# Transposes of x1 as pairs of 64 rows, and the issue of loads and stores exchanged between GpSimd and SyncE

## The reference, cut to what matters

```python
x = x + L0_conv(gn(x))     # 3x3 convolution of int8-valued x and weights, with bias
x = x + L1_conv(gn(x))     # keep 2*16 x 16 low frequencies of rfft2, mix channels, irfft2
```

## Time and profile before

| what | value |
|---|---|
| median of 3 runs | 3610.84 (3604.45 to 3612.75) |
| the profiled execution, its own time | 3599.9 |
| its span | 3598.1 |
| TensorE, matmuls busy | 3060.9 (85%) |
| VectorE busy | 3091.9 (86%) |
| ScalarE busy | 2371.9 (66%) |
| GpSimd busy (DMA issues among it) | 695.4 (19%) |
| DMA traffic | 1352.57 MB, mean 376 GB/s |
| chain that ended last, largest parts | TensorE 44%, DMA 41%, VectorE 6% |

### The profile page before, as it was taken

One profiled execution on the slowest core, in us unless ns is written; L12 is line 12 of the kernel. 1 busy time (PEld: TensorE's weight loads), 2 busy tenths in 40 slices (PEclk: granted clock), 3 DMA queues, 4 the chain that ended last, 5 costly groups with the idle time before them and its releaser, 6 DMA issues.

```text
span 3598.1 us, 81875 instructions
## 1 busy us (share of the span) xinstructions
PE 3060.9 (85%) x33273; PEld 1524.8 (42%) x33273; DVE 3091.9 (86%) x3288; ACT 2371.9 (66%) x3523; POOL 695.4 (19%) x1040
## 2 busy tenths in 40 slices
PE   5666666599999999999999999688888888888886
PEld 1111111266666666666666666433222222222222
DVE  6999999998898989898898989399888888888887
ACT  6888888689898888889898988433333333333332
POOL 0000000144344444444443444000000000000000
PEclk7777777799999999999999999799999999999998
DMA  9999999899999999999999999499999999999998
GB/s 398 421 422 421 421 421 421 271 362 362 308 351 341 347 331 344 344 346 356 317 366 312 356 335 327 159 384 427 427 427 427 427 427 427 427 427 427 427 423 370
DMA packets 342542, 1352.57 MB, mean 376 GB/s; under 512 B 45792, under 2 KB 47040, under 8 KB 243808
## 3 DMA queue, kind: packets, MB, share of 16 engines
q1 hardware_dynamic: 223104, 811.13, 60.0%
q0 software_dynamic: 82272, 268.58, 20.4%
q10 hardware_dynamic: 36864, 268.45, 17.7%
HBM read 811.10 MB, written 536.87 MB: 375 GB/s over the span
## 4 chain that ended last, share of the span: by engine, by line
PE 44%; DMA 41%; DVE 6%; ACT 4%; issue 3%; SPq 1%; DVEq 0%; ACTq 0%
DMA out<-ring 20%; PE ps L732 18%; PE ps L743 13%; DMA ring<-x_scratch 9%; DMA ring<-in_x 8%; PE ps L753 7%; DMA x<-in_x 3%; ACT area L320 3%; DVE ring L669 3%; PE ps L694 2%; DMA mixb<-in_x 1%; DVE stat L485 1%; PE ps L770 1%; PE ps L777 1%; DMA vbuf<-in_x 1%
## 5 line engine op out<-in xcount | busy, mean ns | idle before, releaser
L296 POOL DMA_DIRECT2D x_scratch<-ring x1024 | 689.4, 680 | 1565.1 <-DVE ring L580 1543.3
L884 PE MATMUL ps<-x,gj_s 128*128 128x512 bf16 x3072 | 772.8, 405 | 210.7 <-DVE ring L669 209.7
L580 DVE SCALAR_TENSOR_TENSOR ring<-ps,sc,ring 128x1024 f32<-128x1024 f32 x512 | 650.5, 1282 | 158.1 <-PE ps L732 151.3
L669 DVE TENSOR_TENSOR ring<-ps,ring 128x1024 f32<-128x1024 f32 x512 | 603.0, 1219 | 157.5 <-DMA ring<-x_scratch 154.6
L732 PE MATMUL ps<-area,wq 128*32 128x512 bf16 x12264 | 716.8, 381 | 13.7 <-DVE area L575 8.7
L345 ACT ACTIVATE area<-ps 128x512 f32<-128x512 f32 x1024 | 556.2, 599 | 182.5 <-PE ps L743 176.3
L884 PEld LDWEIGHTS ps<-x,gj_s 128*128 128x128 bf16 x3072 | 294.4, 102 | 766.8 <-DVE ring L669 438.5
L485 DVE TENSOR_REDUCE stat<-area 128x1 f32<-128x4096 f32 x128 | 565.3, 4416 | 45.1 <-ACT area L320 44.2
L743 PE MATMUL ps<-id_s,ring 128*128 128x128 f32 x4096 | 559.6, 280 | 6.5 <-ACT area L345 4.2
L352 ACT ACTIVATE area<-ring,qtab 128x2048 bf16<-128x2048 f32 x256 | 517.0, 2019 | 0.0
L743 PEld LDWEIGHTS ps<-id_s,ring 128*128 128x128 f32 x4096 | 441.5, 141 | 162.1 <-issue 153.6
(11 more groups left out here) (137 smaller groups left out, 2187.3 us busy)
## 6 DMA issues: line engine op xcount, KB each, us to landing
ring<-in_x SPq DMA_DIRECT2D x1024, 256.0 KB, 7.4
x_scratch<-ring POOLq DMA_DIRECT2D x1024, 256.0 KB, 6.7
ring<-x_scratch SPq DMA_DIRECT2D x256, 1024.0 KB, 11.0
out<-ring ACTq DMA_DIRECT2D x256, 1024.0 KB, 25.8
ring<-in_x SPq DMA_DIRECT2D x148, 1024.0 KB, 20.3
vbuf<-in_x SPq DMA_DIRECT2D x36, 1024.0 KB, 21.0
mixb<-in_x SPq DMA_DIRECT2D x36, 1024.0 KB, 21.1
x<-in_x SPq DMA_DIRECT2D x36, 1024.0 KB, 21.1
```

The source lines that it names most:

```text
L296: pool.dma_start(x1_rows[b, m, r], xslot(t % XS)[32 * r:32 * r + 32, :].rearrange("p (g w) -> p g w", g=4)).then_inc(s_x_out[t % XS], 16)
L580: nc.vector.scalar_tensor_tensor(out=half, in0=ps[0][:, h * HF:(h + 1) * HF], scalar=col(26), in1=half, op0=ALU.mult, op1=ALU.add).then_in ...
L669: nc.vector.tensor_tensor(half, ps[0][:, hj * 2 * HW:(hj + 1) * 2 * HW], half, ALU.add).then_inc(s_add, 1)
L884: last = mm(bank(j), gj_s[:, (j * 3 + v) * 128:(j * 3 + v + 1) * 128], (z12, z12, z13)[v][:, k % 2], start=(v == 0), stop=(v == 2))
```

## The change

Transposes: each 128x128 transpose becomes two of 64 rows (partitions 0 to 63 and 64 to 127 of the chunk), with a 64x64 piece of the identity, whose 64 columns go to two different banks (4 and 5). Two quarters of the width fill both banks, and ScalarE empties both with two copies before the next two quarters may begin. s_t and s_te count pairs of quarters, two per chunk where it was four. TensorE's loop is reordered: conv's halves stand apart, each behind a pair of quarters. GpSimd now issues the loads of x with their waits, and SyncE the stores of x1, followed by what it did before.

```diff
@@ SyncE @@
-            def load(t):
...
-            for t in range(1, T - XS + 1):
-                sp.wait_ge(s_x_out[(t - 1) % XS], ((t - 1) // XS + 1) * 64)
-                sp.wait_ge(s_t, 4 * t)
-                sp.wait_ge(s_ss, t)
-                load(t + XS - 1)
+            for t in range(T):
+                sp.wait_ge(s_ev, 2 * t + 2)
+                for r in range(4):
+                    sp.dma_start(x1_rows[b, m, r],
+                                   xslot(t % XS)[32 * r:32 * r + 32, :].rearrange("p (g w) -> p g w", g=4)
+                                   ).then_inc(s_x_out[t % XS], 16)
@@ GpSimd @@
-            for t in range(T):
...
-                    pool.dma_start(x1_rows[b, m, r],
+            def load(t):
...
+            for t in range(1, T - XS + 1):
+                pool.wait_ge(s_x_out[(t - 1) % XS], ((t - 1) // XS + 1) * 64)
+                pool.wait_ge(s_t, 2 * t)
+                pool.wait_ge(s_ss, t)
+                load(t + XS - 1)
@@ ScalarE @@
-                act.activation(xt[:, t % 2, v], bank(4 + v % 2), ACT.Copy).then_inc(s_te, 1)
+                for k in range(2):
+                    last = act.activation(
+                        xt[:, t % 2, 2 * pair:2 * pair + 2].rearrange("p v (g k m) -> p k (v g) m", g=4, k=2)[:, k],
+                        bank(4 + k).rearrange("p (s m) -> p s m", m=64), ACT.Copy)
+                last.then_inc(s_te, 1)
@@ TensorE @@
-                if 4 * t + v >= 2:
-                    pe.wait_ge(s_te, 4 * t + v - 1)
+                if t or v:
+                    pe.wait_ge(s_te, 2 * t + v // 2)
                 for g in range(4):
-                    last = nc.tensor.transpose(bank(4 + v % 2)[:, 128 * g:128 * g + 128],
-                                               xslot(t % XS)[:, g * HW + 128 * v:g * HW + 128 * v + 128], id_s[:])
-                last.then_inc(s_t, 1)
+                    for k in range(2):
+                        c0 = 256 * (v % 2) + 64 * g
+                        last = nc.tensor.transpose(bank(4 + k)[:, c0:c0 + 64],
+                                                   xslot(t % XS)[64 * k:64 * k + 64,
+                                                                 g * HW + 128 * v:g * HW + 128 * v + 128],
+                                                   id_s[64 * k:64 * k + 64, 64 * k:64 * k + 64])
+                if v % 2:
+                    last.then_inc(s_t, 1)
...
+                if 2 <= i and i - 2 < T:
+                    conv(i - 2, 0)
                 if small and j < 4:
                     turn_rows(b, 2 * j)
-                if 2 <= i and i - 2 < T:
-                    conv(i - 2, 0)
-                    conv(i - 2, 1)
                 if 4 <= i and i - 4 < T:
                     turn_x1(i - 4, 2)
                     turn_x1(i - 4, 3)
+                if 2 <= i and i - 2 < T:
+                    conv(i - 2, 1)
```

More of the change, by code:

```diff
@@ L257, in _ @@
             last = max(t for t in range(T) if 4 <= t % XS < 8)
-            sp.wait_ge(s_t, 4 * (last + 1))
+            sp.wait_ge(s_t, 2 * (last + 1))
             sp.wait_ge(s_ss, last + 1)
@@ L262, in _ @@
                 sp.wait_ge(s_x_out[k], len(range(k, T, XS)) * 64)
-            sp.wait_ge(s_t, 4 * T)
+            sp.wait_ge(s_t, 2 * T)
             sp.wait_ge(s_ss, T)
@@ L290, in _ @@
             pool.dma_start(brow[:], bias.rearrange("c o -> o c")).then_inc(s_wl, 16)
-            for t in range(T):
+            def load(t):
                 b, m = divmod(t, TB)
-                pool.wait_ge(s_ev, 2 * t + 2)
                 for r in range(4):
-                    pool.dma_start(x1_rows[b, m, r],
-                                   xslot(t % XS)[32 * r:32 * r + 32, :].rearrange("p (g w) -> p g w", g=4)
-                                   ).then_inc(s_x_out[t % XS], 16)
+                    pool.dma_start(xslot(t % XS)[32 * r:32 * r + 32, :].rearrange("p (g w) -> p g w", g=4),
+                                 x_rows[b, m, r]).then_inc(s_x_in[t % XS], 16)
+            for t in range(XS):
+                if t < 8 and t % 2 == 0:
+                    pool.wait_ge(s_sq, max(n for n in range(NT) if n % NGS == t // 2) + 1)
+                load(t)
+            for t in range(1, T - XS + 1):
[3 more added lines that the diff above has]
+                load(t + XS - 1)
         NWL = (6 + 4 + 1) * 16
@@ L339, in scaled, with turned @@
                                scale=qtab[:, B + b:B + b + 1]).then_inc(s_ua, 1)
-            def turned(t, v):
-                act.wait_ge(s_t, 4 * t + v + 1)
-                if t >= 2 and v == 0:
+            def turned(t, pair):
+                act.wait_ge(s_t, 2 * t + pair + 1)
+                if t >= 2 and pair == 0:
                     act.wait_ge(s_w, t - 1)
-                act.activation(xt[:, t % 2, v], bank(4 + v % 2), ACT.Copy).then_inc(s_te, 1)
+                for k in range(2):
[3 more added lines that the diff above has]
+                last.then_inc(s_te, 1)
             def squared(t):
@@ L391, in _ @@
                     turned(i - 4, 0)
-                    turned(i - 4, 1)
                     squared(i - 4)
@@ L396, in _ @@
                 if 4 <= i and i - 4 < T:
-                    turned(i - 4, 2)
-                    turned(i - 4, 3)
+                    turned(i - 4, 1)
                 if small and j == 12:
@@ L739, in turn_x1 @@
                     pe.wait_ge(s_ev, 2 * t + 2)
-                if 4 * t + v >= 2:
-                    pe.wait_ge(s_te, 4 * t + v - 1)
+                if t or v:
+                    pe.wait_ge(s_te, 2 * t + v // 2)
                 for g in range(4):
-                    last = nc.tensor.transpose(bank(4 + v % 2)[:, 128 * g:128 * g + 128],
-                                               xslot(t % XS)[:, g * HW + 128 * v:g * HW + 128 * v + 128], id_s[:])
-                last.then_inc(s_t, 1)
+                    for k in range(2):
[6 more added lines that the diff above has]
+                    last.then_inc(s_t, 1)
             def along_w1(t):
-                pe.wait_ge(s_te, 4 * t + 4)
+                pe.wait_ge(s_te, 2 * t + 2)
                 if t >= 4 and t % 4 == 0:
@@ L765, in turn_rows @@
                 elif n == 1:
-                    pe.wait_ge(s_te, 4 * T)
+                    pe.wait_ge(s_te, 2 * T)
                 else:
```

## The result

| | before | after |
|---|---|---|
| median of 3 runs | 3610.84 | 3665.25 (3664.52 to 3666.03) |
| ratio to before, 95% interval | | 1.0154 (1.0134 to 1.0174) |
| span of the profiled execution | 3598.1 | 3664.2 |
| convolution stage, first to last addition of x1 | 1572 | 1634 |

What follows compares the result with a forecast made beforehand. TensorE was taken to bound the convolution stage, with VectorE pacing next: eight batches saving 8.0 us each give 64, less 2 given back, so 3599.9 - 64 + 2 = 3538 profiled, 3549 as median; range 3505 to 3602.

Steps and rivals of the forecast that it cites:

- the price of a pair: Convolution stage on TensorE: two 64-row transposes cost 0.06 us together, so a block takes 0.63 and saves 0.39.
- the second rival: TensorE transposes: the array halves don't overlap, blocks stay at 1.02 to 1.1 us, time about 3615; chance 0.14.
- the one of weight loads one after another: TensorE transposes: weight loads follow at 0.11 us each, a block takes 1.9, time about 4050; chance 0.05.
- banks and order: Convolution stage: filling and emptying both banks together makes TensorE wait for no copies on a plain chunk.
- TensorE's plain chunk falls from 5.77 to 4.99: Convolution stage: two transpose blocks save 0.78 us of TensorE's time in a chunk without extra steps.
- VectorE at 5.45: Convolution stage: VectorE then paces plain chunks at 5.45 us, a gain of 0.32 on 5.77.
- the clock stays at 1.00: TensorE's granted clock should stay at 1.00; if waits let it fall, every step would be longer than costed.
- queues exchanged: GpSimd loads, SyncE stores: urgent work isn't queued behind load issues, and the loop of nine slots gains about a microsecond.
- its rival: Convolution stage: the exchange slows DMA, stores alone on SyncE's queue at 228 GB/s, time about 3690; chance 0.11.
- My 5.7 a chunk: Convolution stage: assumed DMA limit of 5.7 us a chunk, between 5.91 and the best stretch's 5.55.
- the first rival: Convolution stage: DMA keeps its 355 GB/s, every chunk takes at least 5.91 us, time near 3566; chance 0.25.
- About ten of 32 chunks gain nothing: Convolution stage: about ten of 32 chunks already run at VectorE's pace of 5.38 us, so 22 gain 0.32 each.

Runs made afterwards that it cites:

- e11: Kernel before with only the new order of TensorE's work (both banks filled before the copies), 128-row transposes, old queues: 3605.02 us, ratio 0.9994.
- e2: Kernel before with only the load and store queues exchanged: 3607.26 us, ratio 0.9992.
- e6: Changed kernel, exchanged queues kept, with 64-row pairs only for quarters 0 and 1 of each chunk, 128-row transposes for the rest: 3602.28 us, ratio 0.9978.
- e5: Changed kernel with old queues and 64-row pairs only for quarters 0 and 1 of each chunk, 128-row transposes for the rest: 3582.08 us, ratio 0.9926.
- e1: Changed kernel with the old queues, so new transposes, banks and order without the exchange: 3621.53 us, ratio 1.0036.
- e3: Changed kernel with only 8 of 16 transpose pairs a chunk after the first chunk, 192 instructions a chunk: 3561.93 us, ratio 0.9862.
- e9: Changed kernel with old queues, one of four loads (after nine chunks) and one of four stores; inverse stage reads x: 3481.93 us, ratio 0.9657.
- e7: Changed kernel with two of four stores a chunk left out, inverse stage reading x: 3608.12 us, ratio 0.9989.
- e8: Kernel before with two of four stores a chunk left out, inverse stage reading x: 3592.45 us, ratio 0.9956.

## Why the prediction was wrong, point by point

**Right: the price of a pair.** A block of 16 takes 0.64 to 0.65 against 0.63, a plain chunk of TensorE's work 0.65 + 1.41 + 0.65 + 1.41 + 0.87 = 4.99 against 4.99. That the sum fits to the hundredth is luck: the convolution in two halves is 0.11 longer than in one piece (2.71), and the width transform, now behind a convolution, 0.14 shorter (1.01). The halves overlap: the second rival (0.14) is out, and so is the one of weight loads one after another (0.05). The two loads of a pair start 3 ns apart in the trace, and the next pair follows some 60 ns later, the spacing taken from the earlier trace rows. (Those rows show the first two loads of a block; the later loads of 128 rows there follow at 109 ns, one per transpose of 0.11.) The Trainium skill's 107 ns for 128 columns ("TensorE: Matmul & The Clock Gate", "LDWEIGHTS (loading the stationary operand)") is not what this transposing load shows; the trace decides.

**Right: banks and order at nothing.** e11 shows it to 0.1%. In the changed kernel TensorE's loads wait 0.5 us on average for the copies (74.1 in 162), more than the nothing forecast, but e11 has such waits too (94.5 in 213) and loses no time by them.

**Right: the mixing weights stay hidden.** From the last addition to the first product of mixing it is 2349.7 - 2321.1 = 28.6, before 2291.2 - 2258.8 = 32.4.

**Wrong: "TensorE's plain chunk falls from 5.77 to 4.99", "VectorE at 5.45".** This is the step that failed. I took the engine's work for its pace, and counted 16 removed transposes and 32 added ones as time on the array alone. Each is a matmul and a weight load, so a chunk has 32 instructions more, and these must be fetched. At 5.45 a chunk, 224 instructions need a packet every 254/224 x 5.45 = 6.2 us; before, 192 in 6.15 needed one every 8.1. Where TensorE had run dry, the next packet took 5.45 to land and 1.4 more to its first instruction (medians of the traces), 6.9 a block: that is 224/254 x 6.9 = 6.1 for a plain chunk where I had 5.45. With the small steps, 59648/256 = 233 instructions on average, it is 6.3; the stage measures 1634/256 = 6.38. That takes the whole gain. The count could be read in the page of the kernel before, in the row q8 with its 237 packets, but I had not asked of each engine how it gets its instructions; what a packet takes when it is late, that page does not show.

**Wrong: the clock stays at 1.00.** It was 0.98 over the stage, some 0.02 x 1633 = 33 us of full-speed time. These are not 33 us of loss on top: where the next block is late, slower work only shortens the gap before it. My text named the way: waits let the clock fall. Stretches of the changed kernel at a step of the spectra (L791), whose 128 small matmuls and their weight loads are a whole packet's worth:

```profile
1187.00:1190.00 3.00, 1.00 (x63) 1.00 (x66) 1.53 (x3) 0.00 (x0) 0.00 (x0) 0.71 1.03 288
1190.00:1194.00 4.00, 2.97 (x79) 2.06 (x72) 0.00 (x0) 2.18 (x3) 0.00 (x0) 0.79 0.96 341
1194.00:1197.00 3.00, 1.24 (x16) 0.80 (x17) 0.57 (x1) 0.88 (x2) 0.00 (x0) 0.68 0.12 37
1197.00:1200.00 3.00, 3.00 (x37) 1.31 (x38) 0.71 (x1) 2.21 (x3) 2.00 (x4) 0.50 0.13 46
```

and the chain there:

```profile
1185.23 0.60 PE ps L791 x30
1185.84 3.16 issue
1188.99 1.73 PE ps L791 x84
1190.73 1.05 PE ps L747 x16
1191.78 1.20 PE ps L734 x20
1192.97 2.79 issue
1195.76 0.62 PE ps L734 x4
1196.38 1.05 PE ps L747 x15
1197.43 2.71 PE ps L734 x19
```

After gaps of 3.16 and 2.79 the granted clock falls, in the last stretch it is 0.50 (1.2 of 2.4 GHz); the transposes take 1.05 in place of 0.65 and half a convolution 2.71 in place of 1.41. In the six microseconds from 1194 the DMA queues move only 37 to 46 GB/s.

**The exchange, "queues exchanged" and its rival.** I took some gain from it and gave a loss 0.11, with stores at 228 GB/s on SyncE's queue. The rival's 3690 is near what came, but for the wrong reason. Loads alone move 224 GB/s on GpSimd's queue as they did 228 on SyncE's, and stores alone on SyncE's are faster than either. The changed kernel, loads alone from 666 to 690, stores alone from 703 to 706, columns as in rows 1:

```profile
666.00:690.00 24.00, 8.60 (x69) 3.84 (x73) 18.36 (x53) 6.19 (x6) 12.55 (x23) 0.50 1.03 224
...
703.00:706.00 3.00, 2.66 (x72) 1.92 (x68) 2.93 (x4) 2.29 (x4) 1.54 (x3) 1.00 1.05 395
```

So the 228 belonged to the loads, not to the queue, and the stores, also of 32 partitions at a time, don't share it. e2 shows no cost at 192 instructions; e6 20 and the changed kernel 44, at 208 and 224: only a TensorE that is short of instructions notices the exchange. How it makes more packets late (50 in e6 against 25 in e5, 160 against 106 in e1) stays open.

**DMA as the next limit.** My 5.7 a chunk was never put to the test. Where TensorE was least in the way with full traffic, e3, the queues moved 348 GB/s, 5.98 a chunk, and the time was 3562, close to the first rival's 3566. So with fetch solved, I would now expect that rival and not the forecast's 3549; no run with all of the work and all of the traffic shows it.

**"About ten of 32 chunks gain nothing".** With neither limit (e9) the stage fell by 121, not 64 (and not the 85 that I gave compute alone). A wrong count of VectorE-bound chunks is not enough to explain that: with a gain in all of them it would be 8 x (32 x 0.32 + 1.0) = 90. VectorE's pace was 5.39 and not 5.45, and e9 took away the waits for loads too; no run tells the parts apart.

What stays open is where the instruction packets wait. Their own transfer lasts 1.07 to 1.10 us (median) in e9 as in both kernels, so they are delayed before it starts. After a gap the next one lands 5.45 us later in the changed kernel, 5.44 in e1, 5.3 in e7 and 2.5 in e9 (five gaps only), so much less traffic helps and a quarter less hardly. Traffic is not all: e8 has as little as e7, and there it is 3.4 (nine gaps). No run put the traffic between 99 and 253. Nor did I try to shorten TensorE's program elsewhere, for instance with the stage's code in a loop.

## What to carry to other kernels

Before splitting a TensorE instruction into several, count instructions a microsecond, matmuls and weight loads together, not only array time: here some 37 a microsecond (254 in 6.7 to 6.9 us) were to be had beside full DMA traffic, and splitting all transposes asked for 41. Put another way, a block of 256 whose work takes less than about 6.9 us, the time that a late block took here beside such traffic, no longer hides the fetch of the next. The sign in a profile is an engine idle with "issue" in the middle of a group of equal instructions, at even intervals whatever code runs, and always at the same place when the instructions are counted by 256. Then split only as much as the fetch allows: half of the split, with the queues left alone, gave 3582, 0.7% under the kernel before (a quarter of it gave the same), where all of it lost 0.4%, and 1.5% with the queues exchanged.

## What was not expected of the hardware

- The data traffic delays the instructions. Where TensorE runs short, a 16 KB packet of its program comes every 6.7 to 6.9 us on average beside 311 to 338 GB/s, though its transfer takes 1.1; beside 99 GB/s it came every 6.1, as fast as it was asked for. The first instruction out of it starts 1.2 to 1.7 us after it has landed, and only one block is brought ahead. The Trainium skill, "Runtime: NRT & Kernel Launch", section "Instruction fetch mechanics", says that instructions come in blocks of 16 KiB, 256 instructions, and that crossing a block is "mostly hidden". The size agrees with the 254 counted here; hidden it was at 192 instructions a chunk (gaps of 13 us in the stage), not at 224 (175 us), unless the traffic was small (e9, 4 us).
- Which queue issues loads and which stores is worth nothing in itself (0.9992), but with 224 instructions a chunk it makes 160 packets late instead of 106.
- Two 64-row weight loads for different halves of the array start 3 ns apart; 16 transposes of 64 rows take 0.65, where eight of 128 rows took 1.02.
